# Layer 1's projection with split operands, and the end of the kernel shared between two engines

## The reference

```
x = _layernorm(x + _L0_gnn_ref(x, adj, ...))   # A_hat mix, two linear maps, two batch norms
x = _layernorm(x + _L1_gnn_ref(x, ..., adj, src, dst))
x = _layernorm(x + _L2_gnn_ref(x, adj, adj, W1, W2, W3))   # three mixes with adj*adj
x = _layernorm(x + _L3_gnn_ref(x, adj, W, a))   # dense attention
# layer 1, the one that changes most
Xq = (H @ W_lin.T).reshape(bt, n, h, dh)
Xv = (H @ W_val.T).reshape(bt, n, h, dh)
e = einsum('behd,hd->beh', leaky_relu(Xq[:, src] + Xq[:, dst], 0.2), a) + log(A0[src, dst] + EPS)
attn = softmax of e over the edges of one src
Y = segment_sum(attn * Xv[:, dst], src);  return Y @ W_out.T
```

## Time and profile before

| | |
|---|---|
| time, three runs | 548.84, 549.05, 550.1 us; median 549.05 |
| the profiled execution | 549.37 us; its span 547.6 us |
| mean granted clock of PE | 0.988 |
| busy share of the span | PE 95%, PEld 86%, DVE 76%, ACT 68%, POOL 35% |
| chain that ended last | PE 83%, DVE 12%, ACT 2% |

### The profile page before, as it was taken

The page is one execution under the profiler, slowest core; times in us unless marked ns, Lnnn a source line. Parts: engine busy times, 40 slices in busy tenths (PEclk is TensorE's granted clock), DMA queues, the critical chain, the costliest instruction groups (busy, mean ns, idle before and its releaser), DMA issues.

```text
span 547.6 us, 11188 instructions
## 1 busy us (share of the span) xinstructions
PE 522.4 (95%) x3684; PEld 471.8 (86%) x3684; DVE 416.9 (76%) x1463; ACT 370.5 (68%) x768; POOL 192.8 (35%) x239
## 2 busy tenths in 40 slices
PE   7999999889999999999999999999999999999964
PEld 6988635779999899989989989989999998989953
DVE  4899677988795663588787787687788676788797
ACT  4776694737775534366687686785786787686774
POOL 4980261444516405027136037027116115210203
PEclk9999999989999999999999999999999999999987
DMA  7631000435434300000001000100100100100002
GB/s 189 182 89 56 0 0 4 125 104 161 148 117 128 104 2 0 1 1 2 2 0 40 0 1 5 33 0 0 38 0 0 38 1 0 38 2 1 21 20 77
DMA packets 34180, 23.72 MB, mean 43 GB/s; under 512 B 2992, under 2 KB 32816, under 8 KB 34144
## 3 DMA queue, kind: packets, MB, share of 16 engines
q1 hardware_dynamic: 32144, 17.58, 10.9%
q0 software_dynamic: 1712, 5.44, 3.3%
q10 hardware_dynamic: 288, 0.26, 0.1%
HBM read 14.88 MB, written 8.39 MB: 42 GB/s over the span
## 4 chain that ended last, share of the span: by engine, by line
PE 83%; DVE 12%; ACT 2%; issue 1%; POOL 1%; POOLq 0%; DVEq 0%; ACTq 0%
PE psum L292 16%; PE psum L293 15%; PE psum L294 15%; PE psum L2176 10%; PE psum L1964 5%; PE psum L2023 4%; PE psum L2031 3%; PE psum L2118 2%; PE psum L2128 2%; PE psum L2040 2%; PE psum L2222 2%; PE psum L2204 2%; PE psum L1891 1%; DVE soft L1116 1%; PE psum L2196 1%
## 5 line engine op out<-in xcount | busy, mean ns | idle before, releaser
L208 POOL TENSOR_TENSOR ln_r<-ln_v,mhalf 128x8 f32<-128x8 f32 x25 | 41.0, 1641 | 220.1 <-DVE ln_v L202 220.1
L2176 PE MATMUL psum<-l2w_s,h 128*128 128x128 f32 x512 | 59.8, 275 | 0.0
L2176 PEld LDWEIGHTS psum<-l2w_s,h 128*128 128x128 f32 x512 | 59.0, 192 | 0.6
L292 PE MATMUL psum<-qt_hi,l2w_s_hi 128*128 128x512 f32 x128 | 52.7, 412 | 0.0
L294 PE MATMUL psum<-qt_hi,l2w_s_lo 128*128 128x512 f32 x128 | 50.6, 395 | 0.0
L293 PE MATMUL psum<-qt_lo,l2w_s_hi 128*128 128x512 f32 x128 | 50.5, 395 | 0.0
L286 ACT ACTIVATE keep_x<-keep_x,ln_b,ln_r (+1 forms) x104 | 42.7, 488 | 2.6 <-POOL ln_b L211 2.6
L1691 ACT ACTIVATE h<-psum 128x512 f32<-128x512 f32 x60 | 34.8, 593 | 11.7 <-PE psum L294 11.6
L292 PE MATMUL psum<-wgt_hi,h_hi 128*128 128x256 f32 x128 | 37.2, 290 | 1.1 <-DVE h_lo L1093 0.9
L293 PE MATMUL psum<-wgt_lo,h_hi 128*128 128x256 f32 x128 | 35.8, 279 | 0.0
L294 PE MATMUL psum<-wgt_hi,h_lo 128*128 128x256 f32 x128 | 35.7, 279 | 0.0
(11 more groups left out here) (297 smaller groups left out, 1751.6 us busy)
## 6 DMA issues: line engine op xcount, KB each, us to landing
keep_x<-in_x SPq DMA_DIRECT2D x32, 128.0 KB, 3.1
xin<-in_x SPq DMA_DIRECT2D x32, 128.0 KB, 2.4
v_rows<-vst SPq DMA_DIRECT2D x32, 128.0 KB, 2.0
out_x<-ob SPq DMA_DIRECT2D x24, 128.0 KB, 1.8
out_x<-keep_x SPq DMA_DIRECT2D x8, 128.0 KB, 2.0
l2w_raw<-in_l2w POOLq DMA_DIRECT2D x1, 512.0 KB, 5.3
adjs<-in_adj_t ACTq DMA_DIRECT2D x2, 128.0 KB, 2.5
adjs<-in_adj SPq DMA_DIRECT2D x2, 128.0 KB, 3.0
```

The lines of the kernel that those rows point to most:

```text
L208: pool.tensor_tensor(ln.r[:].rearrange("p s k -> p (s k)"), ln.v[:].rearrange("p s k -> p (s k)"), mhalf[:], ALU.pow).then_inc(ln.root, 1)
L292: pe.matmul(o, lhs[0], rhs[0], start=start, stop=False)
L2176: i = pe.matmul(bank(s)[:, 0, k * D:(k + 1) * D], h2[:, s, g, j * N + t * P:j * N + (t + 1) * P], l2w3_s[:, g, :], start=(g == 0), stop=(g ...
```

## The change

- q and v are projected at once: `wvq` and the turned rows are split into high and low parts, and each tile takes three products of 256 columns into one bank. Bank 2+2s holds the tiles of node half t=0 of a slot, the next bank those of t=1, each with v and q of both graphs side by side. POOL splits `wvq` in setup.
- `x1t` has a low part, made by a new DVE operation, `x_low`, for which `project` now waits. `q_low` also waits for `v_out`, the end of ACT's v copy of the same slot.
- In the pairs PE turns the rows ahead of `turn_out`; ACT copies q, v, q, v instead of q, q, v, v, and scales after the turned rows.
- After the last pair, ACT's scale of slot 0 stands ahead of the z copies, and DVE's apply of slot 0 ahead of a low part.
- At the end, `hidden1` of slot 14 and its split are done in two halves; DVE's two `fin_norm` of slot 14 go to ACT (`seventh_scaled`), with two short operations on DVE and two on POOL for their bias; the order of the stores follows; PE has five more `spin` products ahead of a wait.

```
-            return bank(2 + 2 * s + k)[:, 0, :].rearrange("p (t j d) -> p t j d", t=T, j=2)
+            return bank(2 + 2 * s, 2).rearrange("p t (j k d) -> p t j k d", j=2, k=2)[:, :, :, 1 - k, :]
...
+            def x_low(q):
+                dve.wait_ge(xt_hi, q + 1)
+                dve.tensor_tensor(x1t[1][:, q % 2, :], bank(2 + 2 * (q % 2))[:, 0, :], x1t[0][:, q % 2, :], ALU.subtract).then_inc(xt_lo, 1)
             def q_low(q):
                 dve.wait_ge(q_hi, q + 1)
+                dve.wait_ge(v_out, q + 1)
...
             for p in range(2, IT - 2):
                 leaky(p - 1)
+                for s in range(2):
+                    x_low(2 * p + s)
...
-            def project(q, k):
+            def project(q):
-                if k == 0:
-                    pe.wait_ge(xt_out, q + 1)
-                elif q >= 2:
+                pe.wait_ge(xt_lo, q + 1)
+                if q >= 2:
                     pe.wait_ge(v_out, q - 1)
...
-                        i = pe.matmul(projected_bank(q % 2, k)[:, t, j, :], x1t[:, q % 2, c:c + P], wvq[:, 1 - k, :], start=True, stop=True)
-                i.then_inc(v_done if k else q_done, 1)
+                        i = three(pe, bank(2 + 2 * (q % 2) + t)[:, 0, j * 2 * D:(j + 1) * 2 * D], [h[:, q % 2, c:c + P] for h in x1t],
+                                  [h[:].rearrange("p k d -> p (k d)") for h in wvq_s], True, True)
+                i.then_inc(qv_done, 1)
...
             turn_x1(0)
             turn_out_slot(2, 0, False)
-            project(0, 0)
-            project(0, 1)
             turn_x1(1)
+            project(0)
             turn_out_slot(2, 1, False)
-            project(1, 0)
-            select(0)
-            project(1, 1)
+            project(1)
             turn_out(3, False)
+            select(0)
             select(1)
...
             for p in range(1, IT - 1):
+                for s in range(2):
+                    turn_x1(2 * p + s)
                 if 2 <= p < IT - 2:
                     turn_out(p + 2, False)
-                for s in range(2):
-                    turn_x1(2 * p + s)
...
+                turned(p)
                 if p > 1:
                     scale0(p + 1, 0, (1, 3))
-                turned(p)
-                if p > 1:
                     scale0(p + 1, 1, range(4))
                 for s in range(2):
-                    q_high(2 * p + s)
-                for s in range(2):
-                    v_copied(2 * p + s)
+                    projected(p, s)
...
-            for s in range(2):
-                z_copied(Q - 2 + s)
-            for q in range(2):
-                first_scale(act, q, ln1, (1, 3), ln1.one_scaled)
-                xs_high(q)
+            first_scale(act, 0, ln1, (1, 3), ln1.one_scaled)
+            z_copied(Q - 2)
+            xs_high(0)
+            z_copied(Q - 1)
+            first_scale(act, 1, ln1, (1, 3), ln1.one_scaled)
+            xs_high(1)
...
-            for j in range(2):
-                fin_norm(0, j)
...
+            sixth_scaled(0)
+            for j in range(2):
+                end_attended(3, j, 0)
+            for j in range(2):
+                seventh_scaled(j)
+            sixth_scaled(1)
...
+            spin(5, 0)
             pe.wait_ge(ex_ready, 2 * L + 3)
```

More of the change, by code:

```diff
@@ L1021, in _ @@
             leaky_slot(0, 1)
+            x_low(2)
+            x_low(3)
+            q_low(2)
+            q_low(3)
             first_apply(dve, 5, ln0, range(4), ln0_done[1], 2)
@@ L1045, in _ @@
             leaky(IT - 2)
+            for s in range(2):
+                x_low(Q - 2 + s)
             def add(p, s, done, psum_bank, ln):
@@ L1384, in _ @@
             for s in range(2):
-                h1_low(L, s)
+                if s == 0:
+                    for j in range(2):
+                        dve.wait_ge(h1_hi, 2 * L + j + 1)
+                        dve.scalar_tensor_tensor(out=h1[1][:, 0, j].rearrange("p t f -> p (t f)"), in0=bank(j)[:, 0, :], scalar=0.0,
+                                                 in1=h1[0][:, 0, j].rearrange("p t f -> p (t f)"),
+                                                 op0=ALU.max, op1=ALU.subtract).then_inc(h1_lo, 1)
+                else:
+                    h1_low(L, 1, 1)
             variance(M, ln2, False)
@@ L1817, in _ @@
                 pt_high(L, s)
-            for s in range(2):
-                h1_high(L, s)
+            for j in range(2):
+                act.wait_ge(h1_done, 2 * L + j + 1)
+                act.activation(h1[0][:, 0, j].rearrange("p t f -> p (t f)"), bank(j)[:, 0, :], ACT.Relu).then_inc(h1_hi, 1)
+            h1_high(L, 1, 1)
             for s in range(2):
@@ L1880, in _, with seventh_scaled @@
                 i.then_inc(ln3.done, 1)
+            def seventh_scaled(j):
+                act.wait_ge(ln1.one_rstd, 2 + j + 1)
+                for t in range(T):
+                    k = 2 * t + j
+                    y = row(L)(0, t, j)
+                    i = act.activation(y, y, ACT.Identity, bias=ln1.b[:, 0, k:k + 1], scale=ln1.r[:, 0, k:k + 1])
+                i.then_inc(end_scaled, 1)
+            sixth_scaled(0)
+            for j in range(2):
+                end_attended(3, j, 0)
+            for j in range(2):
+                seventh_scaled(j)
+            sixth_scaled(1)
         @block.tensor
@@ L2102, in _ @@
                 for s in range(2):
-                    project(2 * p + s, 0)
-                for s in range(2):
-                    project(2 * p + s, 1)
+                    project(2 * p + s)
                 score_slot(p - 1, 1)
@@ L2139, in mix_x, with hidden1 @@
                 i.then_inc(pt_done, 1)
[L2141 removed]
+            def hidden1(p, s, halves=False):
                 pe.wait_ge(pt_lo, 2 * p + s + 1)
                 for j in range(2):
+                    if halves and j:
+                        i.then_inc(h1_done, 1)
                     for t in range(T):
@@ L2149, in hidden1, with mix_hidden @@
                 i.then_inc(h1_done, 1)
-            def mix_hidden(p, s):
-                pe.wait_ge(h1_lo, 2 * p + s + 1)
+            def mix_hidden(p, s, halves=False, more=0):
+                pe.wait_ge(h1_lo, 2 * p + s + 1 + more)
                 for f in range(GA):
                     for j in range(2):
+                        if halves and f == 0 and j:
+                            pe.wait_ge(h1_lo, 2 * p + s + 2)
                         for t in range(T):
@@ L2371, in _ @@
                     pe.wait_ge(ln2.added, 2 * L)
-                hidden1(L, s)
+                hidden1(L, s, halves=s == 0)
             for s in range(2):
-                mix_hidden(L, s)
+                mix_hidden(L, s, halves=s == 0, more=s)
             for s in range(2):
```

76 lines of the change are left out of this document (40 added, 36 removed).

## The result

The changed kernel takes 562.49 us (median of 4, 561.81 to 563.17) against 548.94 (548.34 to 550.1) in the same session: ratio 1.0244, 95% interval 1.0226 to 1.0263. The forecast was 556.7, range 551.5 to 561.5: the direction was right, the size too small. The medians are 13.55 apart. The profiled execution of the changed kernel is the fastest of its four, 561.81 with a span of 560.0 and a mean granted clock of 0.987 (the others: spans of 560.6 to 561.4, clocks of 0.977 to 0.981). Against the 547.6 of before the profiled spans differ by 12.4; what the other executions take beyond that is in no trace of this kernel.

A forecast was written before the change was run, and what follows sets the result against it. It took PE to bound steady pairs and DVE the front. Front +7.9, steady pairs 0, softmax pair +2.2, step -1.1, tail -1.35 gave +7.65 on the median 549.05: 556.7 us, range 551.5 to 561.5.

The forecast's parts named there:

- the step to layer 2: After layer 1's last pair: slot 0's scale and apply moved ahead shorten PE's wait for xs_low; -1.1 us, bounds -1.6 and 0.
- pair 5: Layer 1, one of the three pairs forecast as steady; no change in time, 0 for the three together.
- the clock in the front: Start of layer 1: turn_out and select(0) run at half speed after a 3.7 us PE wait; +1.4 us.
- The front at full clock: Start of layer 1: low parts and q_low's wait for v delay the chain; +6.5 us before any clock loss.
- half speed in all of the front: Rival: projections of slots 0 to 3 on the path at half speed, up to 5.8 us more; 561.0 with three; 22%.
- A steady pair: Layer 1 pairs: 8.98 us against 9.00, PE's saved 0.8 becoming waits of 0.5 at the turn and 0.4 at the selects.
- Three such pairs: 0: Layer 1's three steady pairs together: no change in time, bounds -1 to +2 us.
- The pair with the softmax: Layer 1's softmax pair: DVE's maxima now stand ahead of two leaky and two low parts; +2.2 us, bounds 0 and +3.
- The tail: Kernel's end: h1 in halves and scales moved off DVE; together -1.35 us, bounds -2 and -0.3.
- The moved scales: Tail: four scales (1.21 us) leave DVE's end and two short operations come in; -1.05 us.
- h1 in halves: Tail: slot 0's h1 in halves removes a wait of 0.94 us, of which 0.3 is left as gain.
- POOL's split: Setup: POOL's split of the weights takes 1 us ahead of a long POOL wait; 0 effect.

The follow-up runs named there:

- e5: Changed kernel with unused products on PE in every wait of the front of over 1.2 us; 559.48 us, ratio 1.0202.
- e6: Changed kernel with ScalarE copying slot 1's turned rows and v earlier in the front, and unused products in PE's front waits; 555.94 us, ratio 1.0136.
- e13: e6 without the low part of the turned rows, so two products a tile instead of three; 549.40 us, ratio 1.0011.
- e14: Changed kernel with take_scores ahead of pair 5's leaky, and two unused PE products ahead of each score of the softmax pair; 560.45 us, ratio 1.0206.
- e8: Changed kernel with take_scores ahead of pair 5's leaky and low parts, and the old order in the step to layer 2; 561.52 us, ratio 1.0237.
- e10: e7 with the sixth pair's second scaling moved into an earlier ScalarE wait and its two stores ahead of the seventh pair's; 547.51 us, ratio 0.9964.
- e7: Kernel before with the changed tail alone; 548.07 us, ratio 0.9992.
- e1: Changed kernel with ScalarE's copy of v of slot 1 moved ahead of the four scales of slots 2 and 3; 560.55 us, ratio 1.0206.
- e12: Changed kernel with all repairs: e6, e8's two undone steps, e10's stores, and the softmax maxima spread over pairs 5 and 6; 555.40 us, ratio 1.0102.
- e9: Kernel before with five unused products on PE ahead of pair 1's first select; 547.12 us, ratio 0.9966.

## Why the prediction was wrong in size

The sum fell 4.75 short of the profiled 12.4. Three of its terms failed: the step to layer 2 (1.39 of the 4.75), pair 5 (1.08) and the clock in the front (1.02). The front at full clock adds 0.63, and the rest is small or cancels.

- **The front, full clock (6.5 forecast): right in mechanism, 7.1 measured** (e5). Each step stands where it was put: counted from the first low part, leaky(0) comes at 12.89 in e5 and project(4) at 28.99; the forecast had 12.8 and 28.8. e6 shows that 2.85 of it is ScalarE's order, as the prediction named it; e13 that some 3.2 is the low parts with their third product.
- **The clock (1.4 forecast): a step that failed, by size.** "Only one of them is longer than the 2.7 us that the old trace shows ahead of a fall" took one row for a rule. Spells came behind waits of 1.4 to 2.3 too, at other places in each execution; in the profiled one the clock cost 2.42 (e5), and 3.9 to 4.4 in two others with the same front code (e14, e8). The rival "half speed in all of the front" gave 561.0, nearest to the result. It put 5.75 on the clock (1.4 and three projections at 4.35); e8's execution, with most of the projections of slots 0 to 3 at half clock, comes near to that, the changed kernel's profiled one doesn't. That its time is nearest is partly luck, since other terms fill the gap.
- **A steady pair (8.98 forecast): right, 9.15.** From start to start PE loses 0.54 at the second turn (0.34 of it the idle time shown) and 0.35 at the second select, in place of 0.8 saved; the forecast had 0.5 and 0.4. "Three such pairs: 0" failed at pair 5: take_scores had slipped behind two low parts on DVE, and turn_scores waits for it on PE ahead of the score and the projections. I had followed the selects and not this wait; it cost 0.9 (e8) of the 1.08. The three pairs together, +1.39, stay inside the bounds of that term.
- **The pair with the softmax (+2.2): right, +2.41.** DVE's maxima do stand ahead of the leaky; at full clock it is +2.14 (e14), the rest is clock, which the forecast did not have here.
- **The step to layer 2 (-1.1): wrong; measured +0.29.** The first slot did come 0.9 earlier behind the last z copy, but PE then waits 1.02 for the second slot's low part (198.59), and that came 0.08 later (e8, before): the second slot's chain sets the end of the step. The other 0.21 is pair 7's length ahead of it. I priced the wait that went and didn't ask what was late next.
- **The tail (-1.35): -1.56 to DVE's last operation, then 0.43 back** because the last store became the third of three in a row (e10). The moved scales gave about 1.07 (1.05 forecast); h1 in halves 0.29 here (0.3) and nothing in e7. Alone on the old kernel the time can't be told from nothing (e7); its trace shows 0.78. No row showed the price of POOL's split; in setup it took 1.45 instead of 1, and the front starts no later.
- **Where the saved PE time went:** nowhere in the time. In the front the shorter projections are on the chain, but the low part ahead of each and the waits for v add more than they save; in the pairs the 0.8 became waits.

## What to carry to other kernels

Before you shorten one engine's work, check what then stands last in each stage: here 0.8 us of PE a pair was bought with two low parts on a VectorE that had no slack where it mattered. Where a buffer layout makes one reader wait for another, move the other reader's work up in its queue in the same edit. Price a moved step by the last slot that passes it, not the first. Where PE works in short stretches between waits, don't price its clock from one row: fill the waits in an experiment, and read more than one execution.

## What the runs showed of the hardware

- The half-clock spells aren't fixed to a place in the program: the same front code had a mean granted clock of 1.00 from 97 to 109 in the changed kernel's profiled execution and stretches of 0.50 there in e8's, and the front took 41.56 and 43.52 us. The mean granted clock of the changed kernel's four executions is 0.977 to 0.987; that of the kernel before lay between 0.986 and 0.991 in the 32 executions beside e1 to e12.
- PE work that nobody uses, put into waits, is worth real time: 2.42 us of front in e5, and in the kernel before 1.12 of front for 2.4 us of unused products (e9, ratio 0.9966). It holds only where it is put: e5's softmax pair, without any, took 12.79 where e14's, with some and nearly the same code, took 11.35.
